# GpSimd's indirect transfers in one numbered order, two in flight at most

## The reference, cut to what matters

```python
h = tokens(x)                              # 65 tokens of 128 images: patches @ W + b, class token, * pos_embed
h = h + lstm(layernorm(h))                 # the recurrence runs over the 65 tokens
xt = layernorm(h).reshape(-1, 128)         # 65 * 128 = 8320 rows of 128
probs = softmax(xt @ router_w.T + router_b)
topk_p, topk_i = lax.top_k(probs, 2)       # two of 16 experts for each row
for e in range(16):                        # dense in the reference: gates are 0 for experts not chosen
    y = gelu(xt @ w1[e].T + b1[e]) @ w2[e].T + b2[e]       # 128 -> 512 -> 128
    out = out + y * gates[:, e, None]
return h + out
```

## Time and profile before

| what | value |
|---|---|
| timed runs, median (lowest, highest) | 675.6 us (674.2, 677.68) |
| span of the profiled execution, which is all that the page gives of its time | 771.4 us |
| PE, DVE, ACT, POOL busy | 84%, 73%, 64%, 54% of the span |
| indirect transfers, lines 1235 and 1257 | 130 and 160 |
| busy time of POOL in them | 149.2 and 157.0 us |
| mean granted clock of TensorE | 0.957 |

### The profile page before, as it was taken

How to read it: one execution, slowest core, us unless ns; L and a number is a source line. 1 busy time by engine, 2 the same in 40 slices (tenths; PEclk the granted TensorE clock), 3 DMA queues, 4 the chain that set the end, 5 groups by cost and what they waited for, 6 DMA issues and landing times.

```text
span 771.4 us, 24553 instructions
## 1 busy us (share of the span) xinstructions
PE 647.2 (84%) x7952; PEld 594.7 (77%) x7952; DVE 562.3 (73%) x1797; ACT 493.0 (64%) x1259; POOL 413.1 (54%) x446
## 2 busy tenths in 40 slices
PE   4999999999999999988877665878888787888870
PEld 4999999999999999888875554766666666666660
DVE  3877888888888888778886444756565756677777
ACT  4678876766667666554446343657666767777783
POOL 0243344777767666655656646545555555545552
PEclk9999999999999999999997767999999999999995
DMA  8987877888888887765522222344323234444555
GB/s 318 372 263 271 277 253 251 261 267 256 276 261 267 276 244 236 236 213 182 162 64 60 71 63 73 108 123 119 111 78 98 78 93 118 138 137 131 170 177 195
DMA packets 71895, 141.67 MB, mean 184 GB/s; under 512 B 13078, under 2 KB 55650, under 8 KB 63838
## 3 DMA queue, kind: packets, MB, share of 16 engines
q1 hardware_dynamic: 62128, 121.69, 50.1%
q0 software_dynamic: 9280, 17.21, 6.4%
q10 hardware_dynamic: 366, 1.21, 0.5%
HBM read 116.35 MB, written 25.66 MB: 184 GB/s over the span
## 4 chain that ended last, share of the span: by engine, by line
PE 25%; DVE 24%; another core or an unknown queue 13%; issue 13%; ACT 4%; POOL 3%; DMA 1%; POOLq 0%; ACTq 0%; DVEq 0%; SPq 0%
PE pair L1279 14%; DVE patches L1099 7%; PE pair L1434 3%; DVE patches L1121 2%; PE pair L1325 2%; POOL sent L1235 2%; ACT pair L680 2%; PE pair L1452 2%; PE pair L1289 1%; DVE patches L1114 1%; DVE h L1172 1%; DVE patches L1107 1%; DVE patches L1132 1%; DVE field L843 1%
## 5 line engine op out<-in xcount | busy, mean ns | idle before, releaser
L1257 POOL DMA_INDIRECT back<-patches x160 | 157.0, 981 | 150.6 <-DVE patches L1114 104.6
L680 ACT ACTIVATE pair<-pair,b1s 128x256 f32<-128x256 f32 x320 | 126.3, 448 | 110.4 <-remote 51.5
L1279 PE MATMUL pair<-field,patches 128*128 128x128 f32 (+1 forms) x1408 | 173.9, 280 | 8.9 <-DMA patches<-in_x 8.6
L1279 PEld LDWEIGHTS pair<-field,patches 128*128 128x128 f32 (+1 forms) x1408 | 164.6, 194 | 9.6 <-issue 8.6
L1235 POOL DMA_INDIRECT sent<-pay,slot_own x130 | 149.2, 1148 | 40.3 <-issue 38.2
L1434 PE MATMUL pair<-patches,ex_hi 128*128 128x256 f16 x640 | 119.4, 280 | 47.8 <-DVE patches L1099 23.8
L605 ACT ACTIVATE gate<-pair,lbias 128x128 f32<-128x128 f32 x260 | 74.4, 369 | 98.1 <-PE pair L1294 88.6
L1452 PE MATMUL pair<-ex_hi,patches 128*128 x1280 | 117.4, 225 | 8.3 <-issue 6.1
L1247 POOL TENSOR_TENSOR rstd<-veps,cst 128x2 f32<-128x2 f32 (+1 forms) x68 | 58.0, 853 | 107.2 <-DVE veps L800 106.6
L1107 DVE CAST patches<-pair 128x256 f16<-128x256 f32 x80 | 33.7, 422 | 109.6 <-remote 105.2
L1434 PEld LDWEIGHTS pair<-patches,ex_hi 128*128 x640 | 56.6, 99 | 72.8 <-issue 64.0
(11 more groups left out here) (150 smaller groups left out, 1257.7 us busy)
## 6 DMA issues: line engine op xcount, KB each, us to landing
patches<-in_x SPq DMA_DIRECT2D x62, 1152.0 KB
patches<-sent SPq DMA_DIRECT2D x80, 130.0 KB
field<-in_we SPq DMA_DIRECT2D x64, 128.0 KB
field<-back SPq DMA_DIRECT2D x10, 768.0 KB
patches<-in_b SPq DMA_DIRECT2D x80, 64.0 KB
field<-in_pos SPq DMA_DIRECT2D x65, 64.0 KB
out_tower<-h SPq DMA_DIRECT2D x10, 384.0 KB
back<-patches POOLq DMA_INDIRECT x160
```

The lines of the kernel that those rows point to most:

```text
L680: last = act.activation(up[:, cols], up[:, cols], ACT.Gelu, bias=b1s[:, bass.ds(e * FC + 2 * half + i, 1)], scale=1.0 / E_SCALE)
L1257: pool.indirect_dma_start(back, bass.IndirectOffsetOnAxis(ap=dsti[j % NO][:, k:k + 1], axis=0), yo[j % NO][:, k, :], None, bounds_check=2 ...
L1279: last = pe.matmul(bank_of, l, w_, start=(c == KS and k == 0), stop=(c == KS - 1 and k == 2))
```

## The change

All 290 indirect transfers get a number k in the order in which GpSimd issues them (`issue_order`). Eight semaphores `landed` take the place of the 24 of `sent_done` and the 12 of `y_out`: transfer k raises number k % 8, and `landing(eng, k)` waits for it. Ahead of transfer k GpSimd waits for the landing of k-2. Whoever waited for all earlier places of a ring now waits for the last two transfers in number (`landed_to`), and VectorE, before it writes a place of `yo` or `dsti` again, for the second half of the tile 11 before.

```diff
 NO = 12
+LANDINGS = 8
+IN_FLIGHT = 2
...
-        sent_done = [sem(f"sent_done{i}") for i in range(NP)]
+        landed = [sem(f"landed{i}") for i in range(LANDINGS)]
...
-        y_out = [sem(f"y_out{i}") for i in range(NO)]
...
+        def issue_order():
+
+            sends, order = send_slots(), []
+            for n in range(-5, AHEAD + TILES_B + 4):
+                order += [("row", t, choice) for t, choice in sends.get(n, ())]
+                j = n - AHEAD - 3
+                if 0 <= j <= TILES_B - 1:
+                    order += [("tile", j, half) for half in range(HALVES)]
+            return {what: k for k, what in enumerate(order)}
+
+        ISSUED = issue_order()
+
+        def landing(eng, k):
+
+            eng.wait_ge(landed[k % LANDINGS], 16 * (k // LANDINGS + 1))
+
+        def landed_to(eng, k):
+
+            for i in range(max(k - IN_FLIGHT + 1, 0), k + 1):
+                landing(eng, i)
...
         def tiles_landed(eng, tiles):
 
-            for q in range(NO):
-                eng.wait_ge(y_out[q], 16 * HALVES * len(range(q, tiles, NO)))
+            landed_to(eng, ISSUED["tile", tiles - 1, HALVES - 1])
+
+        def result_landed(eng, j):
+
+            landing(eng, ISSUED["tile", j + 1, HALVES - 1])
...
         def rows_sent(eng, t):
-            eng.wait_ge(sent_done[t % NP], (t // NP + 1) * 32)
+
+            landed_to(eng, ISSUED["row", t, 1])
...
                     if j == 0:
                         sp.wait_ge(tok_done, (T - 1 - 3))
                         sp.wait_ge(lo_done, (T - 1 - 3))
-                        for t in range(STARTS[EARLY_GROUPS] - NP, STARTS[EARLY_GROUPS]):
-                            rows_sent(sp, t)
+                        rows_sent(sp, STARTS[EARLY_GROUPS] - 1)
                     if j == EARLY:
-                        for t in range(T - NP, T):
-                            rows_sent(sp, t)
+                        rows_sent(sp, T - 1)
...
                     if j >= NO:
-                        dve.wait_ge(y_out[j % NO], j // NO * 16 * HALVES)
+                        result_landed(dve, j - NO)
...
+                    k = ISSUED["row", t, choice]
+                    if k >= IN_FLIGHT:
+                        landing(pool, k - IN_FLIGHT)
                     pool.indirect_dma_start(
                         sent, bass.IndirectOffsetOnAxis(ap=slot_own[:, g % 4, choice, col:col + 1], axis=0),
                         pay[:, t % NP, :], None, bounds_check=E * CAP - 1, oob_is_err=False
-                    ).then_inc(sent_done[t % NP], 16)
+                    ).then_inc(landed[k % LANDINGS], 16)
...
-                    for k in range(HALVES):
-                        pool.indirect_dma_start(back, bass.IndirectOffsetOnAxis(ap=dsti[j % NO][:, k:k + 1], axis=0),
-                                                yo[j % NO][:, k, :], None, bounds_check=2 * TOKENS - 1,
-                                                oob_is_err=False).then_inc(y_out[j % NO], 16)
+                    for half in range(HALVES):
+                        k = ISSUED["tile", j, half]
+                        landing(pool, k - IN_FLIGHT)
+                        pool.indirect_dma_start(back, bass.IndirectOffsetOnAxis(ap=dsti[j % NO][:, half:half + 1],
+                                                                                axis=0),
+                                                yo[j % NO][:, half, :], None, bounds_check=2 * TOKENS - 1,
+                                                oob_is_err=False).then_inc(landed[k % LANDINGS], 16)
```

More of the change, by code:

```diff
@@ L1130, in step_b @@
                     if n >= NO:
-                        dve.wait_ge(y_out[n % NO], n // NO * 16 * HALVES)
+                        result_landed(dve, n - NO)
                     dve.scalar_tensor_tensor(dsti[n % NO], xt[n % 4][:, :, HID + 1], tabj[:, 0, n:n + 1],
@@ L1217, in step @@
                         if g >= 4:
-                            for k in range(STARTS[g - 4], STARTS[g - 3]):
-                                rows_sent(pool, k)
+                            rows_sent(pool, STARTS[g - 3] - 1)
                         m, a = SIZES[g], STARTS[g] % NP
                         pool.tensor_copy(slot_own[:, g % 4, :, 0:m], slotf[:, :, 0:m]).then_inc(ids_done, 1)
-                        for k in range(STARTS[g], STARTS[g + 1]):
-                            if k >= NP:
-                                rows_sent(pool, k - NP)
+                        if STARTS[g + 1] > NP:
+                            rows_sent(pool, STARTS[g + 1] - 1 - NP)
                         pool.tensor_copy(pay[:, a:a + m, HID:ROW], tag[:, STARTS[g]:STARTS[g + 1], :]
```

## The result

Four runs of the changed kernel have a median of 833.62 us (828.59 to 837.2), four of the kernel before 676.64 us (674.2 to 677.92): a ratio of 1.233 [1.228, 1.239], 157 us slower. The forecast was 707 us. The direction was right and the size five times too small.

A forecast was written before the change was run, and what follows sets the result against it. The prediction took TensorE to bound the token recurrence, and GpSimd to become the tile stage's bound. Tiles 30 us, first stage 2, less 0.3 for fewer waits, on 675.6 gave 707 us; range 673 to 745.

The forecast's parts named there:

- the first stage: Token recurrence: delayed second row transfers cost at most 0.4 us in each of 30 slots, 0 to 12 us, taken as 2.
- reaction: On GpSimd, time from a landing's semaphore to the next transfer's start: taken as 0.5 us, between 0.30 and 0.85.
- Slots with three transfers later: Token stage: slots issuing three row transfers have 2 us idle before the reciprocal root, so they lose nothing.
- The covers that the forecast named: Token stage: 0.71 us idle before the reciprocal root and up to 0.85 us less stretching absorb a 1 to 2 us wait.
- slower still: Rival, chance 0.12: first-stage cover fails too, the root 1 us later in 30 slots adds 30 us; 730 to 760 us.
- The term that was mis-sized: Tile stage: landing 2.9 plus reaction 0.5 gives 3.4 us a tile against 3.0, 30 us over some 75 tiles.
- The tail: End of the kernel: fewer SP waits before the last loads save about 0.3 us on the path.
- The pace of 3.0 us for the timed runs: Tile stage before the change: 3.0 us a tile in timed runs, from estimates of 2.93 and 3.1.
- the "remote" waits: Tile stage: VectorE's 105.2 us waiting for "remote" was taken as lost by the profiled execution and not the timed ones.
- the signs named for it: Tile stage: GpSimd idle ended by its own landings, starts evenly 1.6 to 1.9 us apart, VectorE waiting for landings.
- the two numbers that the forecast has for the lost time: Profiled span less timed median, and PE's idle time in five stretches after 310 us: 95.8 us each.
- no change: Rival, chance 0.17: timed landings as quiet as the last, 2.6 us a tile, below 3.0; 675, up to 679 us.

The follow-up runs named there:

- r3: The changed kernel with the cap of two in flight on the 130 row transfers alone, tile transfers as in the kernel before; 731.31 us.
- r1: The kernel before, unchanged, run again for a second profile; 673.61 us.
- r8: The changed kernel, but from the 9th token on SP loads only a third of each patch; 791.42 us.
- r9: The changed kernel, but in the tile stage a tile's first transfer waits for both transfers before it and the second for none; 924.91 us.
- r5: The changed kernel with three in flight, and VectorE waiting for both halves of the tile 12 before; 714.35 us.
- r2: The changed kernel with eight in flight, 16 semaphores, and VectorE waiting for both halves of the tile 12 before; 675.14 us.
- r4: The changed kernel with the cap of two in flight on the 160 tile transfers alone, row transfers as in the kernel before; 766.92 us.

## Why the prediction was wrong in size

**The step that failed** is the first stage: "What is left is at most 0.4 us on L1247 in each of 30 such slots, with PE full and some lookahead behind it: between 0 and 12 us, I take 2." It cost 52.0 us by the first tile write, 57.7 us in r3. The landing itself was in the rows: more than 5.1 us in the earlier trace rows. But the working treated it as one delay, "by 1 to 2 us", to be set against idle time, and not as a chain that closes in every slot. A slot holds two row transfers as a tile holds two, so the forecast's own formula, landing plus reaction against the slot, applied here as well. With the forecast's numbers it gives 5.1 + 0.3 + 0.5 = 5.9 us against 5.72: the right sign, but only some 6 us over 30 slots. Measured, transfers 2 to 60 have a landing of 4.42 us (5.2 to the semaphore) and start 2.25 us after the landing they wait for, 6.7 us for each two; the slots 44 to 60 have a median of 7.3 us (5.7 in r1).

About half of the loss lies where the prediction has "Slots with three transfers later have 2 us of idle time before L1247: nothing." The last root is 54.5 us later than in r1; up to the end of the slots with two transfers it is 28 us, in the slots with three or more another 27. With two in flight, three transfers are one and a half turns of the chain. r8 shows the two kinds apart: with light patch loads the first 28 us are gone and some 9 of the later 27 are left.

The covers that the forecast named were room within one slot. As I read the timelines, a lateness that the chain hands on to the next slot uses such room once; no run tests this by itself. The rival "slower still" named the failing cover, 30 us at a chance of 0.12, and its sign, a slot longer than 5.72 us, is what the trace shows.

**The term that was mis-sized** is the tile: 3.4 us, so 0.4 over the pace and 30 us. Measured over transfers 150 to 284 it is 4.07:

| part of a tile, us | forecast | measured |
|---|---|---|
| start to last packet | 2.6 | 2.63 |
| last packet to the semaphore | 0.3 | 0.46 (median 0.36) |
| reaction | 0.5 | 0.81 (0.76 or 0.85) |
| standing behind the other chain's transfer, or waiting for something else | 0 | 0.17 |
| sum | 3.4 | 4.07 |

The landing agrees, but by luck in part. 2.6 was the mean of two pairs; over transfers 150 to 284 the mean is 2.92 us in the same trace and 3.08 in r1. It came down to 2.63 only under the cap (2.88 at a depth of three, 3.04 at eight; the loads beside it also come faster there). The reaction is two values, 0.76 in 40 and 0.85 us in 50 of the 134 starts, so at the upper bound of the forecast (0.85), of which I had taken the lower half. The mean time to the semaphore was half as long again as the forecast had it.

The last part was missing. GpSimd works in order: where a landing is late, the next transfer, whose own landing is in, can't start until 1.28 us after the late one. In 41 of the 134 starts the transfer before was what held; these came 1.23 us after their semaphore instead of 0.81, which makes 0.13 of the 0.17. The expectation of r9 had put 0.31 us on this part, from the round values 0.37 and 0.76. r9 itself adds up in these terms: 1.31 + 2.61 + 0.43 to the semaphore + 0.85 = 5.20 us, measured 5.19, with no transfer held. At a depth of three 88 of 134 starts were held. Together with a longer time to the semaphore (3.45 us against 3.09) that is how r5 came to 3.34 us a tile; this is read from its trace, and no run took it apart.

**The tail**, 18 us, was forecast as 0.3 us saved. Once GpSimd is the bound, finished tiles wait in the ring (8 or 9 for most of the stage, 7 at the end), and the last loads wait for all of them: 14 transfers after the last write, all of them nearly empty. "DVE, ACT, PE fall behind it once its 12 result buffers are full" was said, but what stands in the ring at the end wasn't added.

**What was right.** The pace of 3.0 us for the timed runs (3.03 in r1). That the "remote" waits belong to the profiled execution. That fewer waits on SP and ScalarE cost nothing (r2). That GpSimd becomes the bound of the tile stage, that its idle time is ended by its own landings, and that VectorE then waits for the ring (L1156, 77.0 us). Of the signs named for it one missed: the starts aren't in an even row 1.6 to 1.9 us apart, but 1.27 and 2.77 us apart by turns (642.37, 643.64, 646.41).

Of the two numbers that the forecast has for the lost time, one matched by accident: r1 has 18.6 us of idle PE between 310 us and its last write, so not all of the 95.8 us was lost time; and of the 100 us between the two spans 13 lie ahead of the first tile write and 87 in the tiles, 1.10 us a tile and not 1.21. The step from 2.93 to 3.0 made up for that.

Of the other rivals, "no change" rested on quiet landings: 2.07 us at the end of the kernel. That transfer, like the 2.11 us of the earlier trace rows, moved next to nothing, so neither is a reading for 64 KB. A better one is in the trace after the change: for 18 full transfers of the tile stage in whose first 2 us the other queues kept the DMA engines under 5% busy, the mean to the semaphore is 2.3 us. The Trainium skill (DMA: Bandwidth & Descriptors, "Anatomy of one DMA — SWDGE (gpsimd) path") gives an estimate of 2.15 us for 64 KB by its formula. The trace agrees for these quiet transfers to 0.15 us; beside loads the means to the semaphore were 3.1 us in the tile stage and 5.2 us in the token stage.

**What stays open**: some 9 us of the 160 that r3 and r4 don't add up to (four runs of the changed kernel alone lie 8.6 us apart), and why single semaphores come late. Of the 134 starts 11 come 2.4 us after their landing with no earlier transfer in the way; in nine of them the semaphore itself came 0.8 to 2.2 us behind the last packet and GpSimd then started within 0.85 us, and in two GpSimd waited on for something the trace doesn't name.

## What to carry to other kernels

A cap on transfers in flight turns latency that nobody waited for into a chain: with two in flight and two transfers in each period, the period can't be shorter than one landing, measured beside the traffic of that stage, plus the reaction, plus what in-order issue adds when landings vary. Work this out for every stage that issues such transfers, the one with a full engine first, and compare it with that stage's period; a lateness that is handed on isn't covered by idle time within one period. Where a cap is wanted, take the depth at which this sum is well under the period: here four cost 0.65% and eight nothing that one run shows, while two cost 23%.

## What the runs showed of the hardware

- An indirect transfer's landing depends on its neighbours. Mean time from its start to its last packet: 1.91 us for 18 full ones of the tile stage after the change with the DMA engines almost free of other queues, 2.35 beside tile loads, 2.63 beside tile and bias loads, 4.42 beside the patch loads (2.81 beside a third of them).
- Its size mattered little: 14 transfers of 0.6 KB in the same quiet took 1.79 us, 0.12 less than those of 64 KB, and a transfer that moves no row still costs a landing.
- An instruction of GpSimd that waits for a landing starts 0.76 or 0.85 us after the semaphore, against 0.30 us between two transfers of which the second needn't wait. The semaphore comes 0.36 us (median) behind the last packet, in single cases up to 2.2.
- One profiled execution can be 15% longer than another of the same kernel (771.4 and 671.8 us), with waits put down to "remote" on one core. A second profile of the unchanged kernel, and the span beside the timed runs, tell it.
